# Layer 0's attention with a second branch woven in: the branch's steps behind its first convolution four steps earlier, taps in 19 rows instead of 23

## The chip, the core and the metric

One core of a Trainium2 chip runs the whole program. The metric is the device time of one execution in microseconds (us). Engines: PE (TensorE, matrix products), DVE (VectorE), ACT (ScalarE), POOL (GpSimd), and SP, whose queue issues the DMA transfers. Each engine takes its own instructions in order; they wait for one another by semaphores.

## What is computed

Two layers over x of 2048 rows and 128 columns, all in float32:

```python
xn = layernorm(x)
x = x + attn0(xn) + experts0(xn)        # 16 causal heads; 2 of 8 experts
xn = layernorm(x)
x = x + branch(xn) + transformer(xn)    # state space branch; 6 local attention layers
```

The branch, which the change is about:

```python
xz = layernorm(x) * gamma + beta  @ W_in.T + b_in
xin, z = xz[..., :256], xz[..., 256:]
xc = silu(depthwise causal convolution(xin, 15 taps) + conv_b)
dt_low, B, C = split(xc @ W_x.T, [8, 24])        # 8 + 16 + 16
delta = softplus(dt_low @ W_dt.T + b_dt)
h = h * exp(delta * A) + delta * B * xc          # a scan over time, 16 states
y = (sum(h * C) + xc * D) * silu(z)
out = y @ W_out.T + b_out + x
```

## The kernel before

The program has two stages with a barrier between them. The first (to about 931 us) is layer 0's attention and experts, the second the transformer. The branch is worked off beside both: its first 1024 time steps beside the first stage, the rest beside the second. Only the first stage is touched.

**Pieces and steps.** The attention goes through 384 pieces. A piece is a tile of 128 queries of one head against up to 1024 keys. The first 128 pieces are the first half of the queries. Then each of 16 heads has 8 pieces against the full first 1024 keys (a square head) and 8 against 128, 256, ... 1024 keys (a triangle). Pieces 128 to 383 make the steps 0 to 127, two pieces a step: a step is an even piece, and what goes with the odd one follows it. So a square head has four steps and its triangle four; steps 40 to 43 are a square, 44 to 47 a triangle, 48 to 51 a square.

**One piece.** PE makes the scores in one of three pairs of PSUM banks (L608, `scores`), DVE takes the rows' maxima (L728, `top`, two pieces ahead), ACT the exponential (L833, `exp`), DVE transposes (L736, `turn_probs`), PE multiplies with the values (L677, `values`). PE may put new scores into a pair only when ACT's exponential has read it. POOL lays out the values of the next head (L956), once PE has finished a head before it. Beside triangles run the experts: PE and ACT (L845) make, POOL weighs and sums (L964 to L971).

**The branch.** Every engine's loop calls its own `branch(j)` for step j, and each engine has its instructions in the order of this written plan; none of them looks at where the others are but through semaphores. The parts, with the steps before:

- `TAP_ROWS` (steps 22 to 44): DVE convolves channels 0 to 127, 15 taps spread over these 23 steps (L762 to L766, the tap into `k.mu[:, 0]`).
- Steps 25 to 39: POOL convolves channels 128 to 255, one tap a step, each a product into `k.work[:, 0]` (L1029) and a sum (L1031); event `conv1` is the end of the last.
- Step 41: POOL copies the last 14 columns (`tail`).
- Step 45: ACT: SiLU of the gates (L895), a wait for `conv0` and `conv1`, SiLU of the convolved input (L898), and the table for exponentials again (L899).
- Step 46: SP loads the transformer's first weights (`wqk0`) over the convolution's input, after `conv0` and `tail`.
- `VISITS`: a visit takes one turn of the three pairs of banks between two pieces: "xd" (step 47; the factors, 40 rows), "dt" (50, 51), "mo" (97, 126), and before them "in" (19 to 25). ACT evicts each one. "xd" goes to `k.xd`, which lay in `k.we`, the experts' weights.
- Step 48: POOL multiplies by D into `y0` (L1063). Step 49: SP writes the factors' rows to DRAM (L565) and waits for it.
- Steps 52 to 54: ACT's softplus (abs, exp, ln, twice, L879 to L883). Steps 54, 55: POOL's `rate`. Step 56: POOL makes `du` (L1067).
- From `FIRST_SCAN` = 59 on, 64 steps: a scan unit each (rows by SP's DMA, L464; decay on ACT, L472; input product on POOL, L481; the scan on DVE, L493; the output on POOL, L509, L511).

Lines on which the argument turns:

```python
        if j == 45:
            A.wait_ge(s("half_act"), at["act"]["in3"])
            A.activation(k.mz, k.mz, ACT.Silu).then_inc(s("half_act"), ev.up("silu_z"))
            A.wait_ge(s("half_dve"), at["dve"]["conv0"])
            A.wait_ge(s("half_pool"), at["pool"]["conv1"])
            A.activation(k.mu, k.mu, ACT.Silu).then_inc(s("half_act"), ev.up("silu_u"))
```

Of the kernel before, what the change touches and what calls it, by code (L numbers as in the profile page):

```python
# [14 lines left out]
P = 128  # L15
# [14 lines left out]
RX = R + 2 * NS  # L30
# [302 lines left out]
class Events:  # L333
# [6 lines left out]
    def up(self, name):  # L340
# [2 lines left out]
        return 1  # L343


VISITS = {8: ("sa", 0), 10: ("out", 0), 17: ("hat", 0), 19: ("in", 0), 21: ("in", 1), 23: ("in", 2), 25: ("in", 3), 47: ("xd", 0), 50: ("dt", 0), 51: ("dt", 1),
          97: ("mo", 0), 126: ("mo", 1)}
FIRST_SCAN = 59
TAP_ROWS = range(22, 45)
COMBINE = {70: (0, 6), 104: (6, 12)}  # L350
COMBINE_LAST = 12
HALF_EVENTS = {
    "pe": [f"{what}{i}" for what, i in VISITS.values()],
    "act": ["sa0", "out0", "hat0"] + [f"in{i}" for i in range(4)]
# [31 lines left out]
for U in range(NU):  # L386
    SLOTS.append(("piece", U, 0))
    if step_of(U) in VISITS:
        SLOTS.append(("visit", *VISITS[step_of(U)]))
SLOT_OF = {U: z for z, (what, U, i) in enumerate(SLOTS) if what == "piece"}  # L390
# [34 lines left out]
def scanned_in(j):  # L425

    if j is None:
        return None
    u = j - FIRST_SCAN
    return u if 0 <= u < UNITS // 2 else None  # L430
# [91 lines left out]
def attention_sp(k):  # L522
    S, d, s = k.sy, k.d, k.sem
    at = {e: k.ev[e].at for e in k.ev}

    def save_values(heads, half):
        S.wait_ge(s("val"), 6 if half else 3)
        tiles = slice(NTH * half, NTH * (half + 1))
        S.dma_start(k.v_d[heads, half].rearrange("h c a n -> (c a) h n"), k.valL[:, heads, tiles, :].rearrange("p h t v -> p h (t v)")).then_inc(s("vd"), 16)

    def stage_values(b):
        h, half, part = BATCH[b]
        if b >= 2:
            S.wait_ge(s("vb"), b - 1)
        for c in range(4):
            S.dma_start(k.staged[WIN * c:WIN * (c + 1), b % 2, :, :], k.v_d[h, part].rearrange("c a n -> a c n")).then_inc(s(f"staged{b % 2}"), 16)

    save_values(slice(0, 2), 0)
    S.wait_ge(s("vd"), 16)
    stage_values(0)  # L540
    stage_values(1)
    save_values(slice(2, H0), 0)
    S.dma_start(k.rotary[:], d["rotary"]).then_inc(s("qks"), 16)
    S.dma_start(k.qks[:].rearrange("p a b -> p (a b)"), d["qks"][0].partition_broadcast(P)).then_inc(s("qks"), 16)
    S.dma_start(k.turn[:], d["turn"]).then_inc(s("fixed"), 16)
    for U in range(NU):
        b, i, j = *divmod(U, NTH), step_of(U)
        if i == 2 and b + 2 < NB:
            if b == 0:
                S.wait_ge(s("vd"), 32)  # L550
                save_values(slice(0, H0), 1)
            elif b == H0 - 1:
                S.wait_ge(s("vd"), 48)
            stage_values(b + 2)
        if j == 26:
            S.wait_ge(s("half_pool"), at["pool"]["first"])
            fetch_tile(k, 0)
            fetch_tile(k, 1)
        elif j == 46:
            S.wait_ge(s("half_dve"), at["dve"]["conv0"])  # L560
            S.wait_ge(s("half_pool"), at["pool"]["tail"])
            S.dma_start(k.wqk[0], d["lwqk"][0, :, :]).then_inc(s("wqk0"), 16)
        elif j == 49:
            S.wait_ge(s("half_act"), at["act"]["xd0"])
            S.dma_start(k.bc_d[:, 0:TH], k.xd[R:RX, :]).then_inc(s("bc_saved"), 16)  # L565
            S.wait_ge(s("bc_saved"), 16)
        u = scanned_in(j + 2) if j is not None else None
        if u is not None:
            for w in range(2):
                unit_row(k, u, w)  # L570
# [250 lines left out]
def attention_act(k):  # L821
    A, s, ps = k.ac, k.sem, k.ps
# [51 lines left out]
    def softplus(step, a):  # L874

        A.wait_ge(s("half_act"), ev.n)
        to = k.work[:, a, :]
        if step == "abs":
            ins = A.activation(to, k.delta[:, a, :], ACT.Abs)  # L879
        elif step == "exp":  # L880
            ins = A.activation(to, to, ACT.Exp, scale=-1.0)
        else:
            ins = A.activation(to, to, ACT.Ln, bias=1.0)  # L883
        ins.then_inc(s("half_act"), ev.up(f"{step}{a}"))
# [5 lines left out]
        A.activation(here, here, ACT.Exp).then_inc(s("weights"), 1)  # L890

    def branch(j):
        if j == 45:
            A.wait_ge(s("half_act"), at["act"]["in3"])
            A.activation(k.mz, k.mz, ACT.Silu).then_inc(s("half_act"), ev.up("silu_z"))  # L895
            A.wait_ge(s("half_dve"), at["dve"]["conv0"])
            A.wait_ge(s("half_pool"), at["pool"]["conv1"])
            A.activation(k.mu, k.mu, ACT.Silu).then_inc(s("half_act"), ev.up("silu_u"))  # L898
            A.preload_act_table_set("natural_log_exp_and_others")  # L899
        elif j == 52:  # L900
            softplus("abs", 0)
            softplus("exp", 0)
        elif j == 53:
            softplus("ln", 0)
            softplus("abs", 1)
        elif j == 54:
            softplus("exp", 1)
            softplus("ln", 1)
        for n, (J, heads) in enumerate(COMBINE.items()):
            if j == J + 1:  # L910
                weights(n + 1, *heads)

    A.wait_ge(s("shift"), 1)
    for z, (what, U, i) in enumerate(SLOTS):
# [16 lines left out]
        j = step_of(U)  # L931
        if j is not None:
            branch(j)
        elif U >= FIRST:
            j = step_of(U - 1)
# [10 lines left out]
def attention_pool(k):  # L946
    G, s = k.gp, k.sem
# [38 lines left out]
    def rate(a):  # L986
        x = k.delta[:, a, :]
        G.wait_ge(s("half_act"), at["act"][f"abs{a}"])
        G.tensor_scalar(x, x, 0.0, None, ALU.max).then_inc(s("half_pool"), ev.up(f"relu{a}"))
        G.wait_ge(s("half_act"), at["act"][f"ln{a}"])  # L990
        G.wait_ge(s("half_pool"), ev.n)
        G.tensor_tensor(x, x, k.work[:, a, :], ALU.add).then_inc(s("half_pool"), ev.up(f"delta{a}"))
# [40 lines left out]
    def branch(j):  # L1033
        if 25 <= j < 25 + KC:
            conv(j - 25)
        if j == 11:
            G.wait_ge(s("acc"), NTH)
            output("out", 0)
        elif j == 13:
            normal(1, k.xn[:, 0:NTH, :], k.acc[:, 0:NTH, :], "xn")  # L1040
        elif j == 16:
            normal(2, k.hat, k.xn[:, 0:NTH, :], "hat")
        elif j == 18:
            G.wait_ge(s("small"), 80)
            here = k.acc[:, 0:NTH, :]
            G.tensor_tensor(here, here, k.xn[:, 0:NTH, :], ALU.add).then_inc(s("half_pool"), ev.up("rest1"))
            G.wait_ge(s("half_pool"), ev.n)
            G.tensor_tensor(here, here, bcast(k.bout[:], 1, NTH), ALU.add).then_inc(s("half_pool"), ev.up("rest2"))
            G.memset(k.mxp[:, :, 0:PAD], 0.0).then_inc(s("half_pool"), ev.up("pad"))
        elif j == 24:  # L1050
            G.wait_ge(s("half_pool"), at["pool"]["xn"])
            G.wait_ge(s("acc"), NTH + 2)
            G.tensor_copy(k.xs[:, 1:NTH + 1, :], k.xn[:, 0:NTH, :]).then_inc(s("half_pool"), ev.up("first"))
        elif j == 41:
            G.wait_ge(s("half_act"), at["act"]["in1"])
            G.tensor_copy(k.tail[:], k.mxp[:, :, TH:TH + PAD]).then_inc(s("half_pool"), ev.up("tail"))
        elif j in (54, 55):
            rate(j - 54)
        elif j == 48:
            G.wait_ge(s("half_pe"), at["pe"]["in3"])  # L1060
            G.wait_ge(s("half_act"), at["act"]["silu_u"])
            for a in range(ET):
                ins = G.tensor_scalar(k.y0[:, a, :], k.mu[:, a, :], k.cols[:, 10 + a:11 + a], None, ALU.mult)  # L1063
            ins.then_inc(s("half_pool"), ev.up("y"))
        elif j == 56:
            G.wait_ge(s("half_pool"), ev.n)
            G.tensor_tensor(k.mu, k.delta[:], k.mu, ALU.mult).then_inc(s("half_pool"), ev.up("du"))  # L1067
            G.wait_ge(s("half_pool"), ev.n)
        for n, (J, (h0, h1)) in enumerate(COMBINE.items()):
            if j == J:  # L1070
                part_shares(h0, h1)
            elif j == J + 2:
                combine(n + 1, h0, h1, H0 + 2 * h1)
# [9 lines left out]
    for U in range(NU):  # L1083
# [3 lines left out]
        j = step_of(U)  # L1087
        if j is not None:
# [5 lines left out]
            if scanned_in(j - 1) is not None:  # L1094
                outputs(scanned_in(j - 1))
            if VISITS.get(j - 1, ("", 0))[0] == "mo":
                output(*VISITS[j - 1])
        if i == 5 and beside(U - 2)[0] == "experts":
# [1112 lines left out]
def build(nc, d, out):  # L2211
    k = Kernel(nc, d, out)
    with ExitStack() as ctx:
# [21 lines left out]
        with ExitStack() as c:  # L2235
# [23 lines left out]
            k.vb, k.staged = sb("vb", [P, 2, HALF, WIN], c=c), sb("staged", [P, 2, 4, NTH * DV0], c=c)  # L2259
            k.oT = k.xn[:, NTH:NTH + 4, :].rearrange("p (b i) n -> p b (i n)", b=2)  # L2260
            k.pick, k.own = sb("pick", [P, WIN], c=c), sb("own", [P, 4], c=c)
            k.xd, k.mo_out = k.we[0:RX, :], k.we[:].rearrange("p (t d) -> p t d", d=P)
            k.bc = k.xe[:].rearrange("p e m -> p (e m)").rearrange("p (w b t) -> p w b t", w=2, b=2)
            k.mu, k.mz = (w[:].rearrange("p h d -> p (h d)")[:, 0:ET * TH].rearrange("p (a t) -> p a t", a=ET) for w in (k.wqT, k.wkT))
            k.mxp = wqk0[:].rearrange("p (a t) -> p a t", a=ET)
# [142 lines left out]
```

## Time and profile before

| | us |
|---|---|
| median of 3 runs | 2578.75 |
| lowest, highest | 2575.7, 2585.78 |
| the profiled execution, device time | 2579.93 |
| its span on the core | 2578.1 |
| mean granted clock of PE, as a share of full | 0.981 |

Busy time of an engine leaves out waits, branches and the issue of DMAs. PE's two clock levels are 1.2 and 2.4 GHz, 0.50 and 1.00 as granted clock. In a time line a row stands for one instruction or for a run of equal ones; the brackets at its end tell how long the engine was idle before it and what ended that. Times are counted from the span's start. A row of busy time by stretch gives the stretch, its length, the busy time of PE, PEld (weight loads), DVE, ACT and POOL with their instructions, PE's granted clock, the DMA engines' share and GB/s.

### The profile page before, as it was taken

How to read it: one execution, taken by the hardware profiler on the slowest of the kernel's cores; microseconds unless marked ns; L12 is line 12 of the kernel's file. 1: busy time of each engine (PE TensorE's matmuls, PEld its weight loads, DVE VectorE, ACT ScalarE, POOL GpSimd, SP SyncE). 2: the span in 40 equal slices, each digit the busy share in tenths (PEclk: the TensorE clock that was granted, in tenths of full speed). 3: DMA queues.
4: the chain of work that ended last, by engine and by line, in shares of the span. 5: the costliest groups of instructions: out<-in, count | busy, mean ns of one | idle time of the engine just before them, and what ended most of it. 6: DMA issues, size and time to landing. Idle time of an engine off the chain costs nothing. (4 is left out here: it accounts for less than half of the span.)

```text
span 2578.1 us, 67512 instructions
## 1 busy us (share of the span) xinstructions
PE 2359.5 (92%) x26742; PEld 1421.1 (55%) x26742; DVE 2272.9 (88%) x2520; ACT 1848.5 (72%) x4093; POOL 1944.9 (75%) x1768
## 2 busy tenths in 40 slices
PE   7999999899898879899899999999999999999997
PEld 4444443333333346566566666666666666666665
DVE  6778879879999988999678999899999999899994
ACT  4566555556666647787678888788888888888883
POOL 2441147947889857777578999799998999899991
PEclk9999999999999989999899999999999999999999
DMA  3000000003232310300212121112211121111101
GB/s 109 9 9 11 9 7 7 20 20 56 58 59 58 59 33 8 98 15 12 66 47 43 31 59 39 37 33 47 49 43 29 40 63 33 35 35 33 30 17 40
DMA packets 171111, 97.22 MB, mean 38 GB/s; under 512 B 97155, under 2 KB 167791, under 8 KB 169263
## 3 DMA queue, kind: packets, MB, share of 16 engines
q1 hardware_dynamic: 170799, 92.91, 15.8%
q8 instruction: 215, 3.52, 0.6%
q14 instruction: 97, 0.79, 0.1%
HBM read 66.91 MB, written 7.08 MB: 29 GB/s over the span
## 5 line engine op out<-in xcount | busy, mean ns | idle before, releaser
L608 PE MATMUL ps<-xnT,qp 128*128 128x512 f32 (+3 forms) x1280 | 562.3, 560 | 11.1 <-ACT prob L833 11.0
L833 ACT ACTIVATE prob<-ps,mneg,shift 128x1024 f32<-128x1024 f32 (+7 forms) x384 | 366.2, 954 | 285.5 <-DVE mneg L728 285.1
L1924 DVE TENSOR_TENSOR area<-ps,tab 128x2048 f32<-128x2048 f32 x192 | 430.5, 2283 | 66.1 <-ACT area L1710 38.7
L728 DVE TENSOR_REDUCE mneg<-ps 128x1 f32<-128x1024 f32 (+7 forms) x384 | 340.0, 886 | 73.7 <-PE ps L608 73.3
L1441 PE MATMUL ps<-wqk,area 128*128 128x512 f32 x768 | 357.2, 607 | 28.0 <-DVE area L1990 23.1
L736 DVE STREAM_TRANSPOSE area<-prob 128x1024 f32<-128x1024 f32 (+7 forms) x384 | 351.5, 916 | 31.1 <-ACT prob L833 24.9
L2111 POOL TENSOR_TENSOR area<-area,rn 128x1024 f32<-128x1024 f32 x192 | 370.5, 1950 | 7.5
L1531 PEld LDWEIGHTS ps<-wvo,area 128*128 128x128 f32 x3072 | 352.9, 192 | 26.1 <-issue 20.9
L1531 PE MATMUL ps<-wvo,area 128*128 128x128 f32 x3072 | 359.6, 275 | 3.3 <-ACT area L1759 3.3
L608 PEld LDWEIGHTS ps<-xnT,qp 128*128 128x128 f32 x1280 | 222.3, 196 | 202.2 <-issue 174.3
L1752 ACT ACTIVATE ps<-ps,nmxl 128x64 f32<-128x64 f32 x1536 | 321.3, 343 | 5.7 <-DVE nmxl L1904 5.5
L1710 ACT ACTIVATE area<-ps 128x1024 f32<-128x1024 f32 x192 | 196.5, 1024 | 105.1 <-PE ps L1441 105.1
L956 POOL TENSOR_TENSOR vb<-staged,own 128x1024 f32<-128x1024 f32 x48 | 90.8, 1892 | 227.3 <-PE ps L677 219.5
L2091 POOL TENSOR_TENSOR area<-area 128x512 f32<-128x512 f32 x192 | 250.9, 1307 | 4.0 <-DVE area L1924 3.6
L2092 POOL TENSOR_TENSOR area<-area 128x512 f32<-128x512 f32 x192 | 252.5, 1315 | 0.0
L1441 PEld LDWEIGHTS ps<-wqk,area 128*128 128x128 f32 x768 | 138.3, 190 | 179.9 <-issue 131.2
L1449 PE MATMUL ps<-ident,area 128*128 128x128 f32 x1536 | 195.4, 280 | 38.2 <-POOL area L2111 24.1
L1930 DVE TENSOR_REDUCE ss<-area 128x32 f32<-128x2048 f32 x96 | 215.5, 2244 | 0.0
L1449 PEld LDWEIGHTS ps<-ident,area 128*128 128x128 f32 x1536 | 175.0, 144 | 47.8 <-issue 29.8
L1456 PEld LDWEIGHTS ps<-kT,area 64*32 64x32 f32 x12288 | 147.3, 106 | 84.3 <-issue 79.5
L1759 ACT ACTIVATE area<-ps 128x1024 f32<-128x1024 f32 x192 | 184.4, 1011 | 11.4 <-PE ps L1497 11.3
L1456 PE MATMUL ps<-kT,area 64*32 64x64 f32 x12288 | 165.5, 225 | 4.9 <-issue 4.0
(276 smaller groups left out, 4351.2 us busy)
## 6 DMA issues: line engine op xcount, KB each, us to landing
xe<-bc_scratch SPq DMA_DIRECT2D x128, 128.0 KB, 3.7
area<-bc_scratch SPq DMA_DIRECT2D x128, 128.0 KB, 4.0
staged<-values_scratch SPq DMA_DIRECT2D x192, 32.0 KB, 1.9
wqk<-lwqk_dram SPq DMA_DIRECT2D x6, 1024.0 KB, 6.4
xp<-xc SPq DMA_DIRECT2D x96, 48.0 KB, 2.8
xc<-xs SPq DMA_DIRECT2D x96, 32.0 KB
wvT<-lwvT_dram SPq DMA_DIRECT2D x6, 512.0 KB, 8.0
wo<-lwo_dram SPq DMA_DIRECT2D x6, 512.0 KB, 10.2
```

The lines of the kernel that those rows point to most:

```text
L608: mm = E.matmul(ps[:, r + o // 512, 0:w], k.qp[:, group % 2, i * P:(i + 1) * P], k.xnT[:, k0 + o:k0 + o + w], start=o // 512 != masked, st ...
L728: V.tensor_reduce(k.mneg[:, U:U + 1], of, X_AXIS, ALU.max, negate=True).then_inc(s("top"), 1)
L736: V.transpose(k.probT[x][:, i * STRIDE[x]:i * STRIDE[x] + nk], k.prob[:, U % 2, 0:nk]).then_inc(s("prob_turned"), 1)
L833: A.activation(k.prob[:, U % 2, 0:nk], ps[:, r:r + 2, :].rearrange("p a b -> p (a b)")[:, 0:nk], ACT.Exp, bias=k.mneg[:, U:U + 1], scale=k ...
L1441: mm = E.matmul(to[:, c, :], k.xcT[:, n % 4, :], k.wqk[l % 2][:, at + 512 * c:at + 512 * (c + 1)], start=True, stop=True)
L1449: mm = E.transpose(to[:, j // 4, j % 4 * P:(j % 4 + 1) * P], k.rot[:, n % 2, w, 0, j * P:(j + 1) * P], k.ident[:])
L1456: mm = E.matmul(to[WIN * w:WIN * (w + 1), o, j * DH:(j + 1) * DH], k.qT[o * DH:(o + 1) * DH, j, WIN * w:WIN * (w + 1)], k.kT[o * DH:(o + 1 ...
L1531: mm = E.matmul(to[:, 0, 0:P], k.mixT[:, c, :, :].rearrange("p w q -> p (w q)"), k.wvo[:, l % 2, c, :], start=c == 0, stop=c == H - 1, ski ...
L1752: ins = A.activation(here, here, ACT.Exp, bias=k.nmxl[:, n % 2, 8 * o + j:8 * o + j + 1])
L1924: V.tensor_tensor(k.rot[:, n % 2, w, :, :].rearrange("p c (h d) -> p c h d", d=DH), bcast(heads(what, n), 1, 2), bcast(k.tab[:, n % FRAME, ...
L2092: G.tensor_tensor(a[:, :, DH // 2:DH], a[:, :, DH // 2:DH], b[:, :, 0:DH // 2], ALU.add).then_inc(s("added_" + what), 1)
L2111: G.tensor_tensor(of, of, bcast(k.rn[:, n % 2, H * w:H * (w + 1)], 2, DH), ALU.mult).then_inc(s("normal_" + what), 1)
```

## The change

Everything behind the first half's convolution is moved four steps up in all five engines' plans: SiLU from step 45 to 41, SP's load of `wqk0` from 46 to 42, "xd" from 47 to 43, POOL's product with D from 48 to 44, the factors' save from 49 to 45, "dt" from 50 and 51 to 46 and 47, softplus from 52 to 54 to 48 to 50, `rate` from 54 and 55 to 50 and 51, `du` from 56 to 52, the first scan from 59 to 55, "mo" from 97 and 126 to 93 and 122. DVE's 15 taps are spread over 19 steps (22 to 40), not 23. POOL's taps and its tail copy keep their steps. `k.xd` moves from `k.we` to `k.work[:, 1]`, since at step 43 the experts' weights are still read, and ACT gets a wait for the save of its rows before softplus writes there.

```diff
-VISITS = {8: ("sa", 0), 10: ("out", 0), 17: ("hat", 0), 19: ("in", 0), 21: ("in", 1), 23: ("in", 2), 25: ("in", 3), 47: ("xd", 0), 50: ("dt", 0), 51: ("dt", 1),
-          97: ("mo", 0), 126: ("mo", 1)}
-FIRST_SCAN = 59
-TAP_ROWS = range(22, 45)
+VISITS = {8: ("sa", 0), 10: ("out", 0), 17: ("hat", 0), 19: ("in", 0), 21: ("in", 1), 23: ("in", 2), 25: ("in", 3), 43: ("xd", 0), 46: ("dt", 0), 47: ("dt", 1),
+          93: ("mo", 0), 122: ("mo", 1)}
+FIRST_SCAN = 55
+TAP_ROWS = range(22, 41)
@@ attention_sp
-        elif j == 46:
+        elif j == 42:
             S.wait_ge(s("half_dve"), at["dve"]["conv0"])
             S.wait_ge(s("half_pool"), at["pool"]["tail"])
-        elif j == 49:
+        elif j == 45:
             S.wait_ge(s("half_act"), at["act"]["xd0"])
@@ attention_act
-        if j == 45:
+        if j == 41:
             A.wait_ge(s("half_act"), at["act"]["in3"])
-        elif j == 52:
+        elif j == 48:
             softplus("abs", 0)
             softplus("exp", 0)
-        elif j == 53:
+        elif j == 49:
             softplus("ln", 0)
+            A.wait_ge(s("bc_saved"), 16)
             softplus("abs", 1)
-        elif j == 54:
+        elif j == 50:
@@ attention_pool
-        elif j in (54, 55):
-            rate(j - 54)
-        elif j == 48:
+        elif j in (50, 51):
+            rate(j - 50)
+        elif j == 44:
-        elif j == 56:
+        elif j == 52:
@@ build
-            k.xd, k.mo_out = k.we[0:RX, :], k.we[:].rearrange("p (t d) -> p t d", d=P)
+            k.xd, k.mo_out = k.work[0:RX, 1, :], k.we[:].rearrange("p (t d) -> p t d", d=P)
```

## Rows read from the trace of the kernel before

**Rows 1.** The page, busy us, share of the span and instructions of each engine.
```profile
PE 2359.5 (92%) x26742; PEld 1421.1 (55%) x26742; DVE 2272.9 (88%) x2520; ACT 1848.5 (72%) x4093; POOL 1944.9 (75%) x1768
```

**Rows 2.** Busy us (instructions) of each engine by stretch, each one or two heads.
```profile
276.80:294.43 17.63, 17.63 (x109) 7.19 (x107) 17.54 (x17) 10.53 (x17) 1.89 (x1) 1.00 0.04 8
294.43:310.54 16.11, 15.82 (x107) 6.61 (x106) 13.38 (x19) 9.40 (x21) 6.89 (x7) 1.00 0.04 9
378.38:399.78 21.40, 21.35 (x120) 8.72 (x118) 13.75 (x19) 11.51 (x26) 6.88 (x7) 1.00 0.03 7
498.07:527.45 29.38, 22.79 (x102) 8.50 (x102) 15.25 (x20) 16.80 (x26) 16.81 (x15) 0.88 0.15 45
527.45:549.98 22.53, 22.53 (x114) 8.90 (x114) 18.11 (x17) 12.40 (x19) 7.53 (x3) 0.92 0.05 12
549.98:567.60 17.62, 15.06 (x105) 6.07 (x104) 12.76 (x18) 14.10 (x28) 12.09 (x5) 1.00 0.04 9
567.60:603.01 35.41, 35.03 (x216) 13.91 (x214) 34.29 (x43) 23.28 (x50) 22.71 (x15) 1.00 0.24 47
603.01:641.97 38.96, 34.66 (x212) 14.21 (x212) 38.80 (x51) 26.16 (x62) 33.90 (x29) 0.96 0.32 60
885.23:907.81 22.58, 17.17 (x117) 7.00 (x109) 22.58 (x26) 13.57 (x27) 16.61 (x13) 0.96 0.21 33
```

**Rows 3.** Time line of ACT around its SiLU, start and duration in us.
```profile
482.21 1.20 ACT L833 ACTIVATE prob<-ps,mneg,shift 128x1024 f32<-128x1024 f32 x1 [1.62 <-DVE mneg L728]
...
504.25 1.28 ACT L895 ACT_TABLE_LOAD   x1
...
507.36 1.89 ACT L898 ACTIVATE wqT<-wqT 128x2048 f32<-128x2048 f32 x1
...
510.57 0.78 ACT L833 ACTIVATE prob<-ps,mneg,shift 128x512 f32<-128x512 f32 x1
```

**Rows 4.** Time line of DVE: one tap, and the transpose behind ACT's SiLU.
```profile
482.45 1.25 DVE L766 SCALAR_TENSOR_TENSOR wqT<-wqk,taps,wqT 128x1024 f32<-128x1024 f32 x1
...
511.47 0.71 DVE L736 STREAM_TRANSPOSE area<-prob 128x512 f32<-128x512 f32 x1 [6.02 <-ACT prob L833]
```

**Rows 5.** Busy time by stretch, behind ACT's SiLU.
```profile
510.57:527.45 16.88, 15.43 (x66) 5.30 (x66) 7.87 (x9) 6.80 (x12) 4.63 (x6) 0.81 0.24 73
512.00:516.00 4.00, 3.98 (x13) 1.40 (x13) 2.35 (x4) 1.87 (x4) 3.69 (x5) 0.50 0.78 236
```

**Rows 6.** POOL: groups of 404 to 507 us (busy, mean ns, idle before), then its time line.
```profile
L1029 POOL TENSOR_SCALAR area<-wqk,taps 128x1024 f32<-128x1024 f32 x14 | 43.6, 3112 | 0.9
L1031 POOL TENSOR_TENSOR wqT<-wqT,area 128x1024 f32<-128x1024 f32 x14 | 34.6, 2469 | 1.2
...
419.89 1.89 POOL L956 TENSOR_TENSOR vb<-staged,own 128x1024 f32<-128x1024 f32 x1 [3.02 <-PE ps L677]
421.76 2.84 POOL L1029 TENSOR_SCALAR area<-wqk,taps 128x1024 f32<-128x1024 f32 x1
...
482.47 3.93 POOL L1029 TENSOR_SCALAR area<-wqk,taps 128x1024 f32<-128x1024 f32 x1
...
504.07 2.35 POOL L1031 TENSOR_TENSOR wqT<-wqT,area 128x1024 f32<-128x1024 f32 x1
```

**Rows 7.** Plain pieces: busy time of eight and of five, and ACT's rest between two.
```profile
284.08:300.22 16.14, 16.14 (x111) 7.03 (x110) 14.79 (x19) 10.10 (x22) 2.93 (x2) 1.00 0.04 8
300.22:310.54 10.32, 10.03 (x66) 3.66 (x65) 8.91 (x11) 5.78 (x12) 3.96 (x5) 1.00 0.01 2
...
286.34 1.20 ACT L833 ACTIVATE prob<-ps,mneg,shift 128x1024 f32<-128x1024 f32 x1 [0.96 <-DVE mneg L728]
```

**Rows 8.** A softplus instruction, POOL's first input product, and the factors' write (L565).
```profile
550.99 1.05 ACT L879 ACTIVATE area<-area 128x1024 f32<-128x1024 f32 x1
...
577.76 1.29 POOL L481 TENSOR_TENSOR area<-wqT,xe 128x512 f32<-128x512 f32 x1 [0.98 <-DMA xe<-bc_scratch]
...
DMA to landing us min/median/max: 2.0/2.0/2.0
```

## What the change will do to the time

> **What bounds the kernel now.** I read the page's engine totals first [rows 1]: PE 92%, DVE 88%, POOL 75% of the span. Averages don't tell what these edits are worth, for they all lie in the second half of layer 0's attention (about 277 to 924 us). There the next question is what one head costs with and without extra work. A head is eight pieces on ACT (the exponentials of L833); heads alternate between a full square of keys and a triangle, and a step is two pieces, so a square head and its triangle are eight steps. [Rows 2] gives heads from the start of one head's first exponential to the next one's. A plain square head takes 17.6 us with DVE busy for all of it but 0.1: DVE bounds it. A plain triangle takes 16.1 us with DVE at 13.4 and PE at 15.8. With a scan in every step a square takes 22.6 us with DVE full, and a square and a triangle together 39.0 where the plain two take 33.7. So any DVE work in a square head is paid in full, and ACT work delays it as soon as it is longer than ACT's rest between two pieces.
>
> The odd one is the head at 498.07: 29.4 us for a triangle. The time line of ACT [rows 3] says why: at 504.25 ACT loads a table (1.28 us), runs SiLU on the gates until 507.4, SiLU on the convolved input (1.89 from 507.36 on), loads a table back, and only at 510.57 does piece 219 follow. DVE's time line [rows 4] has 6.02 us of idleness there, for it waits for that exponential. Then PE's granted clock is 0.50 [rows 5], the lower of its two levels, after the same standstill, and the visit "xd" takes its turn; the five pieces 219 to 224 take 16.9 us [rows 5].
>
> **POOL is the one to look at.** It convolves the other half of the channels, tap after tap. Its time line from 404 on [rows 6] has one idle stretch, 3.02 us before 419.89, and then none until the last tap's sum ends at 504.07 + 2.35 = 506.4. The code gives this last tap to POOL in step 39, but ACT's step 41 began at 482.21 [rows 3], so POOL is over 24 us behind. In the kernel before, ACT asks for it in step 45, when its SiLU on the gates has just ended at 507.4: the wait costs nothing, by one microsecond.
>
> **The change, part by part.** Sums are made on the profiled execution, whose device time was 2579.93 us, 1.2 us above the median of 2578.75.
>
> *SiLU in step 41 instead of 45.* POOL's taps are not moved: they stay in steps 25 to 39. ACT comes to step 41 at 482.2 [rows 3], plus at most 3.8 us, because by step 40 DVE now has done 15 taps where it had 12, and a tap that isn't held up takes 1.25 [rows 4]. ACT loads the table, runs the first SiLU and stands by about 490; it then waits for POOL until 506.4. Behind that wait on ACT is queued every later exponential; DVE's transposes wait for these, PE's scores for the banks that they free. All three stand for some 17 to 20 us. The second SiLU (1.89) and the table (1.28) follow, and piece 211 starts at about 509.7, where before piece 219 started at 510.57. Thus (a) -0.9 us for the clock time, but (b) eight pieces that before ran beside POOL's late taps are now still to be done. They carry no taps any more. The same eight positions in the plain heads, from 284.08 to 300.22, take 16.1 us [rows 7]; POOL's and ACT's expert work in it may cost up to a microsecond less, so 15.1 to 16.1; I take 15.6. Denser taps in steps 22 to 40 cost nothing: their cover is this very wait; without it they would cost nothing either, since the taps of steps 41 to 44 go.
>
> *The restart.* Before, 16.9 us for pieces 219 to 224, against 10.3 for the same five plain pieces [rows 7]: 6.6 us for half clock and "xd". Now "xd" comes in a square head, at the same distance behind the SiLU. The first two exponentials again come back to back, which in a square head saves 0.96 each more, but PE has full squares to score at half clock. Bounds: three pieces' worth of that saving, -3, and half of the 6.6 again, +3; I take (c) -1.0.
>
> *The "dt" visits* go from a square head (22.5 with them, 17.6 without: 4.9 for the two) to a triangle. The nearest triangle with two visits is at 378.38 [rows 2]: 21.4 against 16.1, 5.3. (d) +0.4.
>
> *Softplus* goes from a triangle (17.6 against 16.1: 1.5 us for all six ACT instructions) to a square head. There ACT's rest between pieces is 0.96 [rows 7], and each of three places puts 2.1 us (two instructions of 1.05, rows 8) into it: 3 x (2.1 - 0.96) = 3.4. (e) +1.9, between 0 and 1.9.
>
> *Scans four steps earlier.* The pair of heads at 567.60, which has scans in its second half only, gets them in all: as the pair at 603.01, 39.0 instead of 35.4. (f) +3.6. At the end the square head at 885.23 loses them: 22.6 to 17.6, (g) -5.0. The half of step 55 that gains a scan and the half of step 119 that loses one are of the same kind and cancel. "mo" visits: one exchanges square for triangle, the other triangle for square, 0 by the same rows, within 1 us.
>
> *SP's queue.* The load of wqk0 in step 42 waits for POOL's tail copy, which stands right behind the last tap and one product of values; behind it stand the loads of the next values, which need POOL's next product anyway. The factors' rows are written after "xd"; that write landed 2.0 us after its issue [rows 8]. ACT's new wait for it, in step 49, has all later exponentials behind it, but comes six steps after "xd", over 20 us: 0. If SP were late by that much, its price would be one for one. The other buffer (work, second half) costs nothing: 40 rows of an ACT copy as before.
>
> Sum: -0.9 + 15.6 - 1.0 + 0.4 + 1.9 + 3.6 - 5.0 = +14.6 us; 2579.9 + 14.6 = 2594.5 profiled, 2593.4 beside the median. The stretch behind 931 us doesn't change.
>
> One place where a rule of the Trainium skill bears. POOL's tap products L1029 take 2.84 us as a rule and 3.1 in the mean, its sums L1031 2.35 and 2.47 [rows 6]: 14 x 0.27 + 14 x 0.12 = 5.5 us more than undisturbed. Long ones stand beside a DVE tap: POOL's 3.93 at 482.47 began just behind DVE's of 482.45 [rows 4, 6]. The Trainium skill, "SBUF - State Buffer", section "Who interferes with whom", says that a DVE instruction with two SBUF inputs contends with a GpSimd instruction that reads SBUF and that the later one is blocked for the whole instruction. By it DVE's fourteen two-input taps could cost POOL from nothing to 1.25 us each, wherever they fall.
>
> **Rivals.**
> 1. *Fewer collisions (not slower by half a per cent).* Place: POOL's chain from 420 to 506. With the taps of DVE packed otherwise, POOL meets fewer of them as the second; at best it wins 5.5 us and the last tap ends at 501: +9.1, 2588. It decides from 1.8 us on (2591.6 is the bound of half a per cent). For it: the three DVE taps of steps 41 to 44 are gone from the stretch in which ACT waits. Against: fourteen taps must still fall between 404 and 486, denser than before, and may collide more (up to 14 x 1.25 - 5.5 = 12 us later).
> 2. *No long wait*: ACT finds the last tap done, since POOL is not late. Then only (d) to (g) are left, +0.9: 2580 at the median. Against: POOL's one idle stretch of 3.02 us; it would have to shed 14.6 us, so that the last tap ends by 491.8, before no time is lost at all; from there on the kernel is not slower.
> 3. *Slow restart*: PE stands for 17 to 20 us, longer than before, and stays at the lower level through further square pieces. Priced as a second restart like the one measured, 6.6 us: 2600.
> 4. *The first scan comes late*: in the kernel before, from the start of the square head at 567.60 to the first input product's end at 577.76 + 1.29 it was 11.5 us [rows 8]; the product waited 0.98 of it for its row. Now four triangle steps, 16.1 us, lie in that place, less a scan's lead of about 1.5: some 3 us to spare. If POOL's values come 6 us late, +3: 2596.
>
> **How the numbers follow.** The forecast has 0.65, its own range being 2586 to 2602 (a, c and e with their bounds). Rival 1 has 0.12, rival 2 0.08, rival 3 0.07, rival 4 0.05, and 0.03 goes to a gain that I can't name: with no stall at all the rows offer only (g), 5 us, where half a per cent is 12.9 us. The range 2582 to 2605 takes in all but rival 2, that gain and the tails. Half a per cent (2565.9 to 2591.6) is about what a measurement of this kernel can tell from no change. Three quarters of the forecast lies above 2591.6: slower 0.48 + 0.12 = 0.60; same 0.17 + 0.12 + 0.08 = 0.37; faster 0.03.
>
> **What would show it.** ACT should have one wait of 15 to 18 us before its second SiLU in step 41, ended by POOL's last tap (L1031) at 506 +- 2; DVE and PE idle for the same stretch; the last tap unmoved. The triangle head before 527 should be shorter, the square one that contains the SiLU about 40 us. The head at the end should take 17.6 plus a visit. I am wrong if POOL's last tap ends before 495, if ACT's wait is put down to something else, or if DVE and PE are busy through it.

## The result and the profile after

The kernel after takes 2592.14 us in the median (2589.62 to 2595.37), the one before 2578.75: the ratio is 1.0049, with a 95% interval of 1.0038 to 1.0059. It is slower by half a per cent, 13.4 us between the medians, where 14.6 us and a time of 2593.4 were forecast. The profiled execution took 2594.14 us, 14.2 more than that of before.

ACT's time line answers to [rows 3]:

```profile
488.94 1.28 ACT L895 ACT_TABLE_LOAD   x1
490.24 1.91 ACT L895 ACTIVATE wkT<-wkT 128x2048 f32<-128x2048 f32 x1
...
509.53 1.91 ACT L898 ACTIVATE wqT<-wqT 128x2048 f32<-128x2048 f32 x1 [17.38 <-POOL wqT L1032]
511.45 1.28 ACT L899 ACT_TABLE_LOAD   x1
512.75 1.20 ACT L833 ACTIVATE prob<-ps,mneg,shift 128x1024 f32<-128x1024 f32 x1
```

There was no idle time before L898, the second SiLU, in the kernel before; now there are 17.38 us, and what ended them is POOL's line 1032, the sum of a tap. POOL's own time line has that tap (lines moved by one) and no gap ahead of it:

```profile
504.17 2.84 POOL L1030 TENSOR_SCALAR area<-wqk,taps 128x1024 f32<-128x1024 f32 x1
507.09 2.34 POOL L1032 TENSOR_TENSOR wqT<-wqT,area 128x1024 f32<-128x1024 f32 x1
509.39 1.89 POOL L957 TENSOR_TENSOR vb<-staged,own 128x1024 f32<-128x1024 f32 x1
```

DVE and PE stand with ACT, DVE for 21.08 us where [rows 4] had 6.02, PE for 22.60:

```profile
514.08 1.25 DVE L736 STREAM_TRANSPOSE area<-prob 128x1024 f32<-128x1024 f32 x1 [21.08 <-ACT prob L833]
```

```profile
514.10 3.78 PE L608 MATMUL ps<-xnT,qp 128*128 128x512 f32 x4 [22.60 <-ACT prob L833]
```

Busy time by stretch, cut at the heads' first exponentials as [rows 2]: the square head with the SiLU; its triangle with the "dt" visits; the square with softplus; a plain triangle; the first pair with scans; and the last two heads.

```profile
480.42:527.64 47.22, 24.62 (x117) 9.14 (x116) 21.12 (x19) 17.79 (x23) 30.17 (x17) 0.75 0.09 28
527.64:549.00 21.36, 21.36 (x120) 8.69 (x118) 13.10 (x18) 11.41 (x26) 12.44 (x9) 1.00 0.06 13
549.00:567.85 18.85, 18.08 (x122) 7.33 (x122) 17.63 (x17) 16.16 (x23) 12.11 (x5) 1.00 0.03 7
567.85:582.89 15.04, 14.30 (x103) 5.83 (x96) 12.65 (x18) 9.21 (x21) 7.66 (x3) 1.00 0.23 54
582.89:622.52 39.63, 35.69 (x214) 14.39 (x213) 38.94 (x51) 26.12 (x61) 31.49 (x24) 0.96 0.24 51
904.34:923.55 19.21, 18.37 (x136) 8.76 (x134) 17.76 (x17) 11.00 (x19) 5.62 (x5) 1.00 0.01 2
923.55:936.27 12.72, 12.32 (x98) 5.44 (x98) 11.18 (x16) 7.29 (x17) 1.24 (x1) 1.00 0.01 1
```

The head with the SiLU has 47.2 us for 21.1 us of DVE's work. Behind it the next three heads are shorter than in the kernel before (21.36, 18.85 and 15.04 us for 29.38, 22.53 and 17.62), the pair with the scans is 4.2 us longer (39.63 for 35.41), and the last two heads together are 6.7 us shorter (31.93 for 38.67). The last exponential ends at 936.27 where before it ended at 923.90: the first stage is 12.4 us longer, and the rest of the program, which is the same, 1.8. That rest took anything from 1644 to 1660 us in the profiled executions of this document (the span less the end of the last exponential), so 1.8 us of it mean nothing, and below the end of the first stage is given beside the medians.

### The profile page after: what moved, and what is told of

Same layout as the page of the kernel before. It is cut to its first block and busy times, and to the rows that moved or that the text cites. A ratio compares the mean times of both kernels' runs of the same rounds, so it can differ in the third digit from the quotient of the medians.

```text
span 2592.3 us, 67513 instructions
## 1 busy us (share of the span) xinstructions
PE 2358.5 (91%) x26742; PEld 1420.5 (55%) x26742; DVE 2280.5 (88%) x2520; ACT 1850.5 (71%) x4093; POOL 1949.4 (75%) x1768
```

## The experiments

**Is it POOL's lag?** POOL's taps 8 to 14 shrink to 8 columns, in the kernel after and in the kernel before. (This diff and those below are shortened: the semaphore increments at the ends of lines are left out, and `n` is written where it is used.)

```diff
+        n = TH if t < 8 else 8
-        G.tensor_scalar(part, x[:, t:t + TH], k.taps[:, 1, t:t + 1], None, ALU.mult)
+        G.tensor_scalar(part[:, 0:n], x[:, t:t + n], k.taps[:, 1, t:t + 1], None, ALU.mult)
-        G.tensor_tensor(y, y, part, ALU.add)
+        G.tensor_tensor(y[:, 0:n], y[:, 0:n], part[:, 0:n], ALU.add)
```

> The kernel after, with POOL's taps 8 to 14 cut to 8 of 1024 columns (that part of the convolution is left out); all else as after. It takes some 7 x 5.2 = 36 us off POOL's chain, so POOL is no longer behind. Theory (ACT's wait for POOL's last tap is the whole loss): ACT's wait of 17.4 us in step 41 is gone, and what is left of the change is what the heads behind 527 us showed, about -4: 2572 to 2579 us. Rival (the loss is in the restart, the denser DVE taps or the earlier scans): 2586 or more.

Measured: 2574.73 us, ratio to the kernel before 0.998 (0.9967 to 0.9993). ACT's time line:

```profile
489.48 1.28 ACT L895 ACT_TABLE_LOAD   x1
490.78 1.91 ACT L895 ACTIVATE wkT<-wkT 128x2048 f32<-128x2048 f32 x1
492.60 1.89 ACT L898 ACTIVATE wqT<-wqT 128x2048 f32<-128x2048 f32 x1
494.50 1.28 ACT L899 ACT_TABLE_LOAD   x1
495.80 1.20 ACT L833 ACTIVATE prob<-ps,mneg,shift 128x1024 f32<-128x1024 f32 x1
```

The two SiLUs stand back to back in step 41. The first stage ends at 917.5, 18.8 us before that of the kernel after. So neither the denser DVE taps nor the restart nor the earlier scans make the loss.

> The kernel before, with the same cut of POOL's taps 8 to 14. Theory (POOL's lag costs nothing before, since ACT asks for the last tap a microsecond after it is done): within 3 us of the kernel before, 2576 to 2580 us; at most the 2.9 us for which PE waited for POOL's values fall away. Rival (POOL's collisions with DVE cost DVE time before too): 5 us or more faster, under 2574.

Measured: 2578.50 us, 0.999 (0.9977 to 1.0004), the first stage ending at 924.6 against 923.9. The same 36 us of POOL's work are worth 17 us in one kernel and nothing that can be measured in the other. That is the lag's cover shown from both sides.

**A smaller cut.** Two taps short (columns `8 if t in (8, 9) else TH`), in the kernel after:

> The kernel after with two of POOL's taps (8 and 9) cut to 8 of 1024 columns (that part of the convolution is left out). A dose between after and the run with seven taps short: it takes 2 x (5.2 - 0.5) = 9 to 10 us off POOL's chain. Theory (the wait is paid one for one): the last tap ends at about 500, ACT's wait falls from 17.4 to about 8 us, the time to 2581 to 2584 us. Rival (part of the wait is covered by other waits): less than 6 us faster, 2586 or more.

Measured: 2584.67 us, 1.0019 (1.0007 to 1.0032).

```profile
500.82 1.91 ACT L898 ACTIVATE wqT<-wqT 128x2048 f32<-128x2048 f32 x1 [8.34 <-POOL wqT L1032]
```

The wait fell by 9.0 us and the next square head started 7.7 us sooner (541.35 for 549.00), and the first stage ended 8.7 sooner (927.5); the median, 7.5 under that of after, came just above what was expected. Most of the wait is paid one for one.

**The DVE taps alone**, in the kernel before: `TAP_ROWS = range(22, 41)`.

> The kernel before with one part of the change alone: DVE's taps in 19 steps, not 23. Theory (denser taps are paid back by the steps 41 to 44 that have none): within 3 us of the kernel before. Rival (the 4.6 us that the triangle head at 421 grew by in the kernel after are a loss of their own): +4 to +6, 2583 to 2585 us.

Measured: 2579.66 us, 0.999 (0.9976 to 1.0005). The triangle head at 422 takes 20.2 us here, as in after (20.15), against 15.6 in before; the heads from step 40 on give most of it back, and the stage ends 2.0 us later than in before (925.9), which the medians don't tell from nothing. Of what comes back, 1.6 us lie in the square head with "dt", which ran at full clock here (20.89 us) and at a granted clock of 0.92 in the profiled execution of before (22.53), so the taps themselves are paid back only in part. POOL's last tap ends at 510.48, 4.1 us later than in before, and ACT's second SiLU starts at 510.63, without idle time before it.

**Do DVE's taps slow POOL's?** In the kernel after, DVE's taps 1 to 14 over 8 columns:

```diff
-            ins = V.scalar_tensor_tensor(y, x[:, t:t + TH], k.taps[:, a, t:t + 1], y, ALU.mult, ALU.add)
+            ins = V.scalar_tensor_tensor(y[:, 0:8], x[:, t:t + 8], k.taps[:, a, t:t + 1], y[:, 0:8], ALU.mult, ALU.add)
```

> The kernel after with DVE's taps 1 to 14 over 8 of 1024 columns (that part of the convolution is left out). It prices the collisions of DVE's taps with POOL's. Theory (a DVE tap that comes first costs POOL up to 1.25 us): POOL's tap products fall from 3.29 us in the mean to 2.84 and its sums from 2.49 to 2.35, so its last tap ends about 8 us sooner, at 500 to 502, and ACT's wait grows longer at its start instead, since ACT comes to step 41 up to 10 us sooner. Rival (no contention): POOL's durations stay.

POOL's groups between 403 and 510 us (busy, mean ns, idle before), first in the kernel after, then in this one:

```profile
L1030 POOL TENSOR_SCALAR area<-wqk,taps 128x1024 f32<-128x1024 f32 x14 | 46.0, 3288 | 0.9
L1032 POOL TENSOR_TENSOR wqT<-wqT,area 128x1024 f32<-128x1024 f32 x14 | 34.8, 2486 | 1.2
```

```profile
L1030 POOL TENSOR_SCALAR area<-wqk,taps 128x1024 f32<-128x1024 f32 x14 | 39.8, 2844 | 0.9
L1032 POOL TENSOR_TENSOR wqT<-wqT,area 128x1024 f32<-128x1024 f32 x14 | 33.0, 2355 | 1.2
```

Both fell to their undisturbed length. The last tap ended at 499.6, 9.8 us sooner, of which 14 x 0.444 + 14 x 0.131 = 8.1 are these durations. ACT came to its SiLU sooner too: its wait is still 16.06 us. The single time, 2581.8, is 10 us under after, but hardly by the wait: without DVE's taps the heads ahead of step 40 were shorter, and step 40 began 8.5 us sooner (471.92 for 480.42).

**POOL's taps earlier, nothing left out.** Instead of one tap in each of steps 25 to 39, in the kernel after:

```diff
+POOL_TAPS = {22: (0, 1), 23: (2, 3), 24: (4,), 25: (5,), 26: (6,), 27: (7, 8), **{28 + i: (9 + i,) for i in range(6)}}
-        if 25 <= j < 25 + KC:
-            conv(j - 25)
+        for t in POOL_TAPS.get(j, ()):
+            conv(t)
```

Two more lines go with it, in this run and the next two: the list of POOL's events follows the new order, since the first taps now stand ahead of its copy `first`, and tap 0 waits for the event before it.

> The kernel after with POOL's taps given out earlier: two in each of steps 22 and 23, one in 24 to 26, two in 27, one in 28 to 33, where it had one in each of 25 to 39. Nothing is left out. Theory: POOL fills the 9.5 us of idleness before 401 and the 3.9 before 421 and ends the last tap 10 to 13 us sooner, so ACT's wait falls from 17.4 to 4 to 7 us and the time to 2579 to 2583 us. Rival (ACT's wait isn't what sets the time): 2590 or more.

Measured: 2582.79 us, 1.0011 (1.0000 to 1.0023), as expected, but for another reason. The last tap ended at 486.1, 23 us sooner (10 to 13 were expected), and ACT's wait was gone where 4 to 7 us of it were expected to stay. A new one stood in its place. PE, then ACT:

```profile
474.64 0.86 PE L678 MATMUL ps<-area,vb 128*32 128x256 f32 x8 [4.41 <-POOL vb L958]
```

```profile
479.80 1.10 ACT L834 ACTIVATE prob<-ps,mneg,shift 128x896 f32<-128x896 f32 x1 [6.70 <-DVE mneg L729]
```

POOL's product of the next head's values (L958) was now queued behind the taps packed ahead of it, and the triangle head at 462.6 took 22.7 us instead of 16.1. The next kernel spreads the taps so that this product has room:

```diff
+POOL_TAPS = {22: (0, 1), 23: (2,), **{24 + i: (3 + i,) for i in range(7)}, 32: (10,), 33: (11,), 34: (12,), 36: (13,), 37: (14,)}
```

> The kernel after with POOL's taps two in step 22, one in 23 to 30, one in 32, 33, 34, 36 and 37, so that POOL's next product of values is not queued behind a tap that could wait (with the taps packed as before this one, PE had waited 4.4 us for it and the triangle head at 463 had grown by 6.6). Nothing is left out. Theory: no wait of ACT for the last tap and none of PE for the values; the first stage ends 6 us before that of the kernel before, as it did with POOL's taps cut short (917.5 instead of 923.9): 2571 to 2575 us. Rival (POOL can't serve both in time, one of the two waits comes back): 2579 to 2585.

Measured: 2575.45 us, ratio 0.9978 (0.9967 to 0.999): faster than the kernel before by a fifth of a per cent, and 17 us faster than after. POOL's last tap ended at 490.1 and ACT came to its second SiLU at 491.1, so it didn't wait, again by a margin of one microsecond; PE didn't wait for the values either. The pair of heads ahead of step 40, and then the square head with the SiLU and its triangle:

```profile
439.56:480.69 41.13, 35.23 (x220) 14.33 (x216) 40.86 (x41) 19.99 (x39) 40.10 (x19) 1.00 0.02 5
480.69:529.34 48.65, 43.39 (x232) 17.06 (x228) 33.36 (x37) 29.07 (x45) 28.49 (x21) 0.96 0.11 33
```

The second row has 48.7 us where after has 68.6 (47.22 + 21.36); the first 41.1 for 38.8 (480.42 - 441.58), so the earlier taps aren't quite free. The first stage ends at 917.4.

> The kernel before with the same paced taps on POOL. Theory (POOL's lag cost nothing before): within 3 us of the kernel before. Rival (early taps of POOL are worth something by themselves): faster by 5 us or more, as much as the run beside it.

Measured: 2575.17 us, 0.9982 (0.9969 to 0.9995), and its first stage ends at 919.3. Here I was wrong: the median is under that of the kernel before, clear of the interval, and the stage is 4.6 us shorter. But of these 4.6, 1.6 lie in the square head at 527 and 1.45 in the last one, in each of which the profiled execution of before had a stretch of half clock that this one had shorter or not at all, and 0.5 were there before the first tap (the head at 399 starts at 399.29 for 399.78). The square head at 399 gains 1.8 (19.97 for 21.80) and the heads behind it up to 527 give 0.8 of that back, so what the stage shows of the taps is one microsecond; where the rest of the median's gain comes from stays open. Once the taps are paced, the four steps by themselves are worth 2 us of the stage (917.4 against 919.3) and nothing that the medians can tell (2575.45 and 2575.17). The two runs with seven taps short lie further apart (917.5 and 924.6 in the stage, 2574.73 and 2578.50 in the median, with intervals that overlap), so a gain of a few us from the four steps is neither shown nor excluded.

**The price of the scans.** The kernel after with `FIRST_SCAN = 59` and "mo" at 97 and 126:

> The kernel after with the first scan and the two mo visits back at steps 59, 97 and 126; all else four steps early. It prices the terms for the scans. Theory (earlier scans cost 4.2 us in the pair of heads at 583 and give back 6.8 in the last pair): the pair at 583 is 4 us shorter, the last pair 6.8 longer, in all 2 to 3 us slower than after: 2593 to 2596 us. Rival (moving scans is neutral, the gain at the end is something else): as after, with the last two heads unchanged.

Measured: 2594.75 us, 1.0055 (1.0041 to 1.007). The pair of heads at 584 and the last two:

```profile
584.10:619.50 35.40, 35.02 (x216) 13.92 (x214) 34.28 (x43) 23.29 (x50) 18.18 (x14) 1.00 0.31 48
902.28:924.87 22.59, 18.02 (x123) 7.14 (x121) 22.59 (x26) 13.69 (x28) 16.46 (x13) 0.98 0.14 33
924.87:939.65 14.78, 14.36 (x112) 7.29 (x111) 11.29 (x16) 7.89 (x18) 5.66 (x5) 0.92 0.00 1
```

35.4 for 39.6 and 37.4 for 31.9: earlier scans cost 4.2, as expected, and give back 5.4, where 6.8 were expected.

**The price of the restart.** While PE stands in step 41 it is given matmuls that nobody reads:

```diff
+        if what == "piece" and U == FIRST + 2 * 41 + 1:
+            for n in range(40):
+                E.matmul(ps[:, 7, :], k.ident[:], k.xnT[:, 0:512], start=True, stop=True, skip_group_check=True)
```

> The kernel after with 40 matmuls of 128x512 that nobody reads, into bank 7, while PE stands in step 41: it prices the restart at the lower clock. In after the first scores behind the wait take 3.8 us instead of 2.0 and the xd visit 4.2, at a granted clock of 0.5. Theory (the restart is paid by half clock): the granted clock behind the wait is 1.0, and the square head with the SiLU becomes 2 to 4 us shorter, 44 instead of 47.2. Rival (DVE and the order of the pieces set the restart): under 1 us.

Measured: 2607.38 us, 1.0097 (1.008 to 1.0114). I had mis-sized the filling, and PE came back 11.8 us too late:

```profile
491.44 34.60 PE L707 MATMUL ps<-xnT,ident 128*128 128x512 f32 x80
525.88 1.88 PE L608 MATMUL ps<-xnT,qp 128*128 128x512 f32 x4
527.69 0.53 PE L677 MATMUL ps<-area,vb 128*32 128x192 f32 x8
528.15 3.63 PE L641 MATMUL ps<-wqT,wx 128*40 128x512 f32 x8
```

It still prices the restart at full clock: from PE's first scores (525.88) to the next head's first exponential (536.60) it took 10.7 us, in after 13.5 (514.10 to 527.64). ACT and DVE had a lead here that they don't have in after, but PE had no idle time behind its first scores in either run, and up to the next scores of 1.98 us its own instructions took 6.24 us here (525.88 to 532.12) and 9.06 in after (514.10 to 523.16). That is the whole difference. Half clock is worth 2.8 us there. In after it lasted until about 520:

```profile
516.00:520.00 4.00, 4.00 (x13) 0.91 (x12) 3.66 (x4) 2.12 (x3) 0.00 (x0) 0.52 0.33 139
520.00:524.00 4.00, 4.00 (x17) 1.23 (x16) 1.54 (x2) 1.49 (x3) 0.00 (x0) 1.00 0.00 0
```

With 23 matmuls:

> As the run before it, which overshot: its 40 matmuls took 34.6 us (0.865 each) and kept PE until 525.9, 11.8 us beyond the 514.1 of after. Now 23 matmuls, 19.9 us, from 491.4 to 511.3, some 2.5 us before PE is wanted. Theory (the restart is paid by half clock): granted clock 1.0 behind the wait, the first scores in 2.0 instead of 3.8 us, xd in 3.6 instead of 4.2, and the square head with the SiLU 2 to 3 us shorter than 47.2: 44 to 45; the time 2589 to 2591 us. Rival (DVE and the order of the pieces set the restart): the head stays over 46.5.

Measured: 2589.58 us, 1.0031 (1.0017 to 1.0044). PE was busy until 512.15 and then idle for 2.69 us, and its clock fell all the same:

```profile
512.00:516.00 4.00, 1.31 (x3) 0.66 (x3) 1.19 (x2) 3.94 (x6) 0.17 (x2) 0.88 0.40 88
516.00:520.00 4.00, 4.00 (x14) 0.91 (x14) 3.83 (x5) 1.55 (x3) 0.00 (x0) 0.69 0.51 211
```

The first scores took 3.62 us, "xd" 3.63, the head 46.2 instead of 47.2: one microsecond, short of what the theory expected and more than its rival did, since the filling kept only a part of the restart at full clock. PE's instructions from its first scores to the next ones of 1.98 us took 7.99 us (514.83 to 522.82), 1.07 less than in after, and the head is 1.05 shorter: this agrees with the price of the run before it and adds no more to it.

**A faster tap.** POOL's first tap, in all kernels, takes 1.20 us for 1024 columns; it has two operations, the other fourteen have one and take 2.84. The kernel after with the products in the form of the first:

```diff
-        G.tensor_scalar(part, x[:, t:t + TH], k.taps[:, 1, t:t + 1], None, ALU.mult)
+        G.tensor_scalar(part, x[:, t:t + TH], k.taps[:, 1, t:t + 1], k.xs[:, 0, 0:1], ALU.mult, ALU.add)
```

> The kernel after with POOL's fourteen tap products in the form of its first tap: the same multiplication, and then the addition of a column of zeros as a second operation. Nothing is left out. POOL's first tap, which has two operations with a column each (L1026 of the kernel before), takes 1.20 us for the same 1024 columns for which the products with one operation take 2.84. Theory (the form with one operation is the slow one, and ACT's wait is the loss): the products fall to 1.2 to 1.6 us, POOL's chain ends some 18 to 23 us sooner, ACT's wait of 17.4 us is gone, 2571 to 2577 us. Rival (the first tap is fast for another reason, its start at column 0 or its output): they stay at 2.84 or more and the time at 2590 to 2594.

Measured: 2577.68 us, 0.9992 (0.9979 to 1.0005): the loss is gone with one line. POOL's groups between 403 and 510 us, and its time line with three of the products:

```profile
L1032 POOL TENSOR_TENSOR wqT<-wqT,area 128x1024 f32<-128x1024 f32 x14 | 33.8, 2415 | 1.2
L1030 POOL TENSOR_SCALAR area<-wqk,taps,xs 128x1024 f32<-128x1024 f32 x14 | 24.8, 1770 | 0.9
```

```profile
452.57 1.20 POOL L1030 TENSOR_SCALAR area<-wqk,taps,xs 128x1024 f32<-128x1024 f32 x1
453.85 3.20 POOL L1032 TENSOR_TENSOR wqT<-wqT,area 128x1024 f32<-128x1024 f32 x1
457.15 1.20 POOL L1030 TENSOR_SCALAR area<-wqk,taps,xs 128x1024 f32<-128x1024 f32 x1
458.44 2.35 POOL L1032 TENSOR_TENSOR wqT<-wqT,area 128x1024 f32<-128x1024 f32 x1
460.89 2.05 POOL L1030 TENSOR_SCALAR area<-wqk,taps,xs 128x1024 f32<-128x1024 f32 x1
```

The products take 1.77 us in the mean for 3.29, 21 us less over the fourteen, and the last tap ends at 491.0, before ACT asks for it at 495.9. Part of the gain is spent on collisions: DVE's taps, shortest, median and longest in ns, first in the kernel after, then here:

```profile
L766 DVE SCALAR_TENSOR_TENSOR wqT<-wqk,taps,wqT x14: 1239/1460/2927, 404.1 to 487.0; 128x1024 f32<-128x1024 f32 x14
```

```profile
L766 DVE SCALAR_TENSOR_TENSOR wqT<-wqk,taps,wqT x14: 1257/2362/3369, 404.9 to 491.4; 128x1024 f32<-128x1024 f32 x14
```

The triangle head ahead of step 40 takes 19.9 us here for 16.1 in after, and the first stage ends at 923.9, 6.5 us later than with the paced taps; the medians of the two (2577.68 and 2575.45) have intervals that overlap. Both changes together were not run.

## Why the prediction was right, and where its terms were off

**The cause** held: one wait on ACT, ended by POOL's last tap, with DVE and PE standing. Forecast 15 to 18 us, measured 17.38. Three of the signs that were named beside it came out otherwise. The last tap was to end at 506 +- 2 and ended at 509.4. All three engines were to stand for 17 to 20 us; DVE stood for 21.08 and PE for 22.60. The square head with the SiLU was to take about 40 us and took 47.2. This last figure never fitted the forecast's own terms: they let ACT begin the head at 480.2 (476.38 + 3.8) and, with 36.8 us from piece 211 on less 21.4 for the triangle, end it at 525.1, which is 45 us. Taking away POOL's lag takes away the loss, by half with two taps cut short and wholly with seven, and just so where nothing is left out (paced taps, the two-operation form); the same cut in the kernel before brings nothing that can be measured.

Term by term, in the profiled executions:

| | forecast | measured |
|---|---|---|
| (a) start of piece 211, beside 219 at 510.57 | 509.7 | 512.75 |
| (b), (c), and "dt" of (d): pieces 211 to 224 | 31.5 + 5.3 = 36.8 | 36.25 |
| (e) the square head with softplus | 17.6 + 3.4 = 21.0 | 18.85 |
| the triangle behind it, plain | 16.1 | 15.04 |
| (f) the first pair with scans | 39.0 | 39.63 |
| (g) the last two heads, from 38.7 | 33.7 | 31.93 |

*(a) was 3.1 us too low.* I let POOL's last tap end at 506.4; it ended at 507.09 + 2.34 = 509.4. POOL waited 3.95 us for PE's values where [rows 6] has 3.02, and its tap products took 3.29 us in the mean instead of 3.11, 14 x 0.18 = 2.5 us. The longer products are the collision with DVE's taps. The forecast gave it to rival 1 as a chance of fewer collisions, and denser taps made more. The kernel before with 19 rows shows the same with the DVE taps alone (3.29 us in the mean, the last tap's end at 510.5). A pair of rows of the kernel after shows both ways round:

```profile
421.27 1.89 POOL L957 TENSOR_TENSOR vb<-staged,own 128x1024 f32<-128x1024 f32 x1 [3.95 <-PE ps L677]
423.14 3.81 POOL L1030 TENSOR_SCALAR area<-wqk,taps 128x1024 f32<-128x1024 f32 x1
```

```profile
421.32 2.92 DVE L766 SCALAR_TENSOR_TENSOR wqT<-wqk,taps,wqT 128x1024 f32<-128x1024 f32 x1
```

DVE's tap began 0.05 us behind POOL's product and took 2.92 us instead of 1.25; POOL's next tap began beside it and took 3.81 instead of 2.84. By the rule of the Trainium skill, "SBUF - State Buffer", section "Who interferes with whom", that the later one is blocked, both follow (blocked until the other's end they would take 3.09 and 3.94), and the run without DVE's taps agrees (2.84 and 2.36 in all fourteen).

*(d)* was priced from a disturbed row. Its 4.9 us for two visits in a square head came from the head at 527.45, which has a granted clock of 0.92 in [rows 2]. In the kernel before with short taps, with 19 rows and with paced taps the same head takes 20.89 us at 1.00, so the visits cost 3.3 there.

*(e) was 2.2 us too high.* I charged all of ACT's 2.1 us beyond its rest of 0.96. The head was 18.85, 1.2 over the plain 17.63. DVE was busy for 17.63 of it, as in a plain head (17.54), so it hardly noticed. My reading, not tested by a run of its own: an exponential ends about a microsecond before DVE takes it up, so the piece had twice the slack that I counted.

*The plain triangle was 1.1 too high.* My 16.1 came from the head at 294.43, which carries expert work; from this head on there is none. The same error made softplus in the triangle of before look like 1.5 us, when 17.62 - 15.04 = 2.6. Both together turn (e) from +1.9 to -1.4, outside the bounds of 0 to 1.9 that it was given.

*(g) was 1.8 too small.* The heads' sum includes a stretch at half clock in the profiled execution of before, in the last head (granted clock 0.84):

```profile
907.81:923.91 16.10, 15.91 (x112) 7.87 (x111) 11.37 (x16) 7.89 (x18) 5.66 (x5) 0.84 0.01 1
```

The kernel before with paced taps and the kernel after with late scans show this head at 14.6 and 14.8 us (0.93 and 0.92); the kernel before with 19 rows has it at 16.0 (0.85), so it differs from execution to execution. By the rows of the run with late scans, earlier scans cost 4.2 and give back 5.4.

The errors are +3.1, -0.6, -2.2, -1.1, +0.6 and -1.8; with -0.4 in the heads between they bring 14.6 to 12.2, and 12.4 was the stage's growth. They cancelled in part; the sum came out better than its terms, and that is luck. So is the last bit of agreement in the whole program's time, 14.2 us profiled for 14.6: 1.8 of it come from the part that didn't change. (c), the restart, wasn't told apart from (b) by the time; the first run with PE kept busy gives 2.8 us for its half clock.

**Rivals.** Rival 1 (fewer collisions) went the other way. Rival 2 (no wait) is excluded by the trace. Rival 3 (a slow restart) didn't come: the granted clock was 1.00 again from 520 on, and the run with PE kept busy puts the whole of it at 2.8 us. Rival 4 (a late first scan) neither: the pair with the first scans is 39.6, within 0.7 of the full pair of [rows 2]. ACT's new wait for the factors' rows in step 49 cost nothing: its time line has no idle time there that a DMA ended.

## What to carry to other kernels

A plan that gives every engine a step is a plan, not a clock: before moving a step up, read at what time each engine that it waits for gets there, and subtract. Here one queue was 24 us behind its step, a margin of one microsecond hid it, and moving its consumer four steps up turned it into a wait of 17 us; spreading that queue's work earlier, or a cheaper form of its instruction, undid all of it. Where work is packed into a queue ahead of its time, ask at once what it now stands in front of, as the run with the packed taps shows.

## What the runs showed of the hardware that I had not expected

- Here a DVE tap (two inputs in SBUF) and a POOL instruction lengthened each other by most of the time for which the other was still running, even where both are short: 1.25 to 2.92 us beside a product of 1.89, 2.84 to 3.81 beside that tap, which ended 1.1 us after POOL's product began. Without DVE's taps POOL's fourteen products all took 2.84 us and its fourteen sums between 2.34 and 2.36.
- PE's granted clock fell after an idle time of 2.69 us that followed 20 us of unbroken matmuls (0.88 and 0.69 in the next two stretches of 4 us), and scores at that level took 3.6 us instead of 1.9.
- POOL's multiplication of 128x1024 float32 by a column takes 2.84 us as one operation and 1.20 with an addition of a column behind it. Why is open.
- 40 matmuls of 128x512 float32 in one row took 34.4 us from the start of the first to the start of what came behind them, 0.86 each; two of a piece's scores took 1.91 (480.05 to 481.96 in after), 0.96 each. Why is open; the forty have one stationary tile, a piece's two scores share one and the next piece's have another.
